# Quantizing the down-projection weights later in a cross-attention and FP4 feed-forward kernel

## The reference

```python
def fp4_quant_dequant(x):                     # blocks of 16 along the last axis
    scale = jnp.maximum(jnp.max(jnp.abs(xb), -1, keepdims=True) / 6.0, 1e-12)
    idx = jnp.searchsorted(_MID, jnp.abs(xb / scale))
    return (_GRID[idx] * jnp.sign(xb) * scale).reshape(shape)
def fp4_linear(x, w):
    return jnp.einsum('bsk,nk->bsn', fp4_quant_dequant(x), fp4_quant_dequant(w))
...
corr = jnp.real(jnp.fft.ifft(Qf * jnp.conj(Kf))).mean(axis=(0, 1))   # over all sequences
W_topk, I_topk = jax.lax.top_k(corr, 12); W_topk = softmax(W_topk)
R = sum(w * roll(v, -shift)); x = x + R @ Wout + bout
...
gate = fp4_linear(ln(x), w_gate); y = fp4_linear(ln(x), w_up)       # 256 -> 704
x = x + fp4_linear(silu(gate) * y, w_down)                           # 704 -> 256
```

## Time and profile before

| | us |
|---|---|
| median of 3 runs | 575.65 (574.96 to 576.95) |
| the profiled execution | 575.05 |
| its span, first to last instruction | 573.2 |
| busy: TensorE, VectorE, ScalarE, GpSimd | 466.7, 461.9, 393.3, 282.7 |

### The profile page before, as it was taken

The page is one execution under the profiler, slowest core; times in us unless marked ns, Lnnn a source line. Parts: engine busy times, 40 slices in busy tenths (PEclk is TensorE's granted clock), DMA queues, the critical chain, the costliest instruction groups (busy, mean ns, idle before and its releaser), DMA issues. The chain is left out here.

```text
span 573.2 us, 10039 instructions
## 1 busy us (share of the span) xinstructions
PE 466.7 (81%) x3454; PEld 306.1 (53%) x3454; DVE 461.9 (81%) x742; ACT 393.3 (69%) x666; POOL 282.7 (49%) x365
## 2 busy tenths in 40 slices
PE   5086798704789999999899999999899999999944
PEld 5075687501345565556555555556555565556633
DVE  2899864315799999999899999999899999998760
ACT  2177865535778777788888777788888778776530
POOL 3045351035356666656556666656556666632221
PEclk9689999775989999999999999999999999999987
DMA  9956550043145556555655557645655556544533
GB/s 283 344 170 202 176 186 14 25 102 75 37 97 122 110 122 127 120 106 111 128 118 119 110 123 126 121 107 110 130 116 119 112 115 110 108 88 98 88 78 78
DMA packets 165042, 69.19 MB, mean 121 GB/s; under 512 B 129152, under 2 KB 164736, under 8 KB 164992
## 3 DMA queue, kind: packets, MB, share of 16 engines
q1 hardware_dynamic: 164416, 68.03, 52.2%
q10 hardware_dynamic: 576, 0.53, 0.3%
HBM read 27.90 MB, written 9.18 MB: 65 GB/s over the span
## 5 line engine op out<-in xcount | busy, mean ns | idle before, releaser
L694 PE MATMUL ps<-guT_hi,a_xT 128*128 128x512 f16 (+1 forms) x384 | 140.7, 366 | 55.2 <-DMA a_xT<-ctx_sb 55.2
L405 POOL TENSOR_TENSOR ctx_sb<-h_c,sl 128x704 f16<-128x704 f16 x64 | 96.1, 1523 | 115.8 <-DVE ctx_sb L909 115.8
L704 PE MATMUL ps<-dT_hi,hqT 128*128 128x256 f16 x704 | 132.2, 276 | 12.3 <-DMA hqT<-ctx_sb 12.3
L696 PE MATMUL ps<-guT_hi,a_xT 128*128 128x512 f16 (+1 forms) x384 | 140.3, 365 | 0.0
L695 PE MATMUL ps<-guT_lo,a_xT 128*128 128x512 f16 (+1 forms) x384 | 140.1, 365 | 0.0
L694 PEld LDWEIGHTS ps<-guT_hi,a_xT 128*128 128x128 f16 x384 | 37.7, 98 | 103.7 <-DMA a_xT<-ctx_sb 46.0
L457 ACT ACTIVATE h_c<-y_h 128x1408 bf16<-128x1408 bf16 (+3 forms) x40 | 49.2, 1230 | 61.9 <-DVE y_h L939 36.5
L706 PE MATMUL ps<-dT_lo,hqT 128*128 128x256 f16 x384 | 89.6, 277 | 0.0
L704 PEld LDWEIGHTS ps<-dT_hi,hqT 128*128 128x128 f16 x704 | 69.7, 99 | 25.2 <-DMA hqT<-ctx_sb 13.1
L443 POOL TENSOR_TENSOR xs<-xs,w_raw 128x512 f32<-128x512 f32 x32 | 37.8, 1180 | 79.5 <-issue 49.6
L904 DVE SCALAR_TENSOR_TENSOR hb<-ps,h_in,w_raw 128x704 f32<-128x704 f32 x64 | 60.5, 945 | 4.7 <-PE ps L696 4.6
(11 more groups left out here) (139 smaller groups left out, 868.8 us busy)
## 6 DMA issues: line engine op xcount, KB each, us to landing
w_raw<-a_scratch SPq DMA_DIRECT2D x64, 128.5 KB, 2.6
xs<-in_x_dram SPq DMA_DIRECT2D x16, 512.0 KB, 5.3
ctx_sb<-in_ctx_dram SPq DMA_DIRECT2D x16, 512.0 KB, 4.4
out_dram<-a_xT SPq DMA_DIRECT2D x64, 128.0 KB, 2.0
hqT<-ctx_sb SPq DMA_TRANSPOSE x64, 3.7
w_raw<-in_L_ffn_w_down_dram SPq DMA_DIRECT2D x1, 704.0 KB, 8.1
w_raw<-in_L_ffn_w_gate_dram SPq DMA_DIRECT2D x1, 640.0 KB, 5.9
w_raw<-in_L_ffn_w_up_dram SPq DMA_DIRECT2D x1, 640.0 KB, 7.1
```

The source lines that it names most:

```text
L405: pool.tensor_tensor(hq[:, j % 2, t, FF:2 * FF].rearrange("p (ih r) -> p ih r", ih=IH), h_c[:, :].bitcast(F16).rearrange("p (ih t r) -> p ...
L694: pe.matmul(dst, xt[:, c, :], guT[0][:, c, n0:n1], start=(c == 0), stop=False)
L696: last = pe.matmul(dst, xt[:, KC + c, :], guT[0][:, c, n0:n1], start=False, stop=(c == KC - 1))
L704: pe.matmul(dst, hqT[:, j % 4, c, :], dT_hi[:, c, :], start=(c == 0), stop=False)
```

## The change

Gate and up, and down, are quantized as two parts, each with its own preparation (`w_prepare(part)`), its own largest value over the partitions (`largest(part)` on GpSimd) and its own factors (`w_scales(part)`).

- The load of the down weights is issued after the inputs of all steps, with a semaphore of its own, ahead of the late small loads.
- In the reading stage only the six pieces of gate and up are quantized (`N_GU` = 6).
- Down: `w_prepare(1)` stands on VectorE after the last `evac_qk` and ahead of the sums over Wout. The factors, both `w_segment` and the output factor with `ident_out` stand after the softmax's last operation; both `w_split` on ScalarE behind the eighth evacuation, ahead of the table load. `w_finish` of the two pieces stands at the end of VectorE's steps -2 and -1, `w_hi` on ScalarE in steps -1 and 0 ahead of the pair's normalization, `w_lo` at the end of GpSimd's steps -1 and 0. Their products lie in `d_prod`, a part of the buffer that held ctx.
- TensorE's five fills of down come in the tile loop: two after tile 2's gate and up, three after tile 3's, in turn through banks 6 and 7. ScalarE evacuates all five in step 1, after the SiLU of tile 3 and ahead of the rounding of x.
- The waits for all fills ahead of the products wait for eight; the first down product waits for 13. The small operations on the factors count on `c_steps` instead of `w_steps`.

```diff
-            down_v = w_raw[:, 256 * GU_CH:WCOLS].rearrange("p (c n) -> p c n", n=FF)
-            sp.dma_start(down_v, w_down.rearrange("(c p) n -> p c n", p=P)).then_inc(s["w_loaded"], 16)
             for i in range(2, NQ):
                 load_x(i)
                 load_c(i)
+            down_v = w_raw[:, 256 * GU_CH:WCOLS].rearrange("p (c n) -> p c n", n=FF)
+            sp.dma_start(down_v, w_down.rearrange("(c p) n -> p c n", p=P)).then_inc(s["d_loaded"], 16)
...
+            def largest(part):
+                pool.wait_ge(s["w_steps"], 2 + part * seg_at(N_GU - 1) + part * K_W)
+                pool.partition_all_reduce(w_pow[:, part:part + 1], w_max[:, part:part + 1], P, RMAX).then_inc(s["w_pool"], 1)
...
-            evacuate_weights(act, range(EARLY, len(FILLS)))
+            evacuate_weights(act, range(EARLY, GU_FILLS))
+            w_split(N_GU)
+            w_split(N_GU + 1)
             act.preload_act_table(ACT.Silu)
...
                 if tile_ok(2 * st - LAG - 1):
                     residual(2 * st - LAG - 1)
+                if st in (-1, 0):
+                    w_hi(N_GU + 1 + st)
...
                 if tile_ok(2 * st + 1):
                     silu(2 * st + 1)
+                if st == 1:
+                    evacuate_weights(act, range(GU_FILLS, len(FILLS)))
...
+                if i == 2:
+                    pe.wait_ge(s["w_lo"], len(SEGS))
+                for f in {2: range(GU_FILLS, GU_FILLS + 2), 3: range(GU_FILLS + 2, len(FILLS))}.get(i, ()):
+                    transpose_weights(f)
+                if i == LAG:
+                    pe.wait_ge(s["w_ev"], len(FILLS))
                 if tile_ok(i - LAG):
                     down(i - LAG)
...
+            def w_prepare(part):
+                cols = cols_of(part * N_GU)[0]
+                at = part * (seg_at(N_GU - 1) + K_W)
+                dve.wait_ge(s["d_loaded"] if part else s["w_loaded"], 16 if part else 16 * N_PIECES)
+                dve.tensor_reduce(w_bm[:, cols], w_raw[:, BLK * cols.start:BLK * cols.stop].rearrange("p (b i) -> p b i", i=BLK),
+                                  AX.X, ALU.max, apply_absolute_value=True).then_inc(ws, 1)
...
+            w_prepare(1)
             dve.wait_ge(s["late_loaded"], 32)
...
+            w_scales(1)
+            w_segment(N_GU)
+            w_segment(N_GU + 1)
+            dve.tensor_scalar(inv_out[:, :], w_inv[:, 1:2], h_tmp[:, 1:2], None, ALU.mult).then_inc(cs, 1)
...
+            dve.tensor_scalar(ident_out[:, :], ident[:, :], out_fac[:, 0:1], None, ALU.mult).then_inc(s["id_out"], 1)
...
+                if st in (-2, -1):
+                    w_finish(N_GU + 2 + st)
```

More of the change, by code:

```diff
@@ L50 @@
 AHEAD = 4
-W_FIRST = 0
 SLOT = P // QT
@@ L215, in chunks_of, with product, runs_of, scratch @@
             return w[:, o:o + n].rearrange("p (c ih r) -> p c ih r", ih=IH, r=r)
-        def runs_of(w, g):
+        def product(g):
+            o, n = SEGS[g]
+            return (hb if g < N_GU else d_prod)[:, FF * (g % 2):FF * (g % 2) + n]
+        def runs_of(g):
             o, n = SEGS[g]
             r = RUN_H if n == FF else RUN_X
-            return w[:, FF * (g % 2):FF * (g % 2) + n].rearrange("p (ih c r) -> p c ih r", ih=IH, r=r)
+            return product(g).rearrange("p (ih c r) -> p c ih r", ih=IH, r=r)
+        def scratch(w, g):
+            o, n = SEGS[g]
+            return w[:, FF * max(0, g - N_GU):FF * max(0, g - N_GU) + n]
+        def seg_at(g):
+            return 7 + K_W * g + (7 if g >= N_GU else 0)
+        def scaled_at(g):
+            return seg_at(g) + 1 if g <= N_GU else seg_at(g) - 2
+        def finish_at(g):
+            return seg_at(g) + (2 if g == N_GU else 1)
         def pair_ok(n):
@@ L249, in evacuate_weights @@
                 eng.wait_ge(s["w_tr"], f + 1)
-                src = bank16(f % 4)
+                src = bank16(f % 4 if f < GU_FILLS else 6 + f % 2)
                 if kind == "gu":
@@ L637, in transpose_weights @@
                 kind, part, a, b = FILLS[f]
-                need(pe, s["w_ev"], f - 3)
-                dst = bank16(f % 4)
+                need(pe, s["w_ev"], f - 3 if f < GU_FILLS else f - 1)
+                dst = bank16(f % 4 if f < GU_FILLS else 6 + f % 2)
                 if kind == "gu":
@@ L668, in _ @@
             pe.matmul(bank(4)[:, 0:P], ones[:, :], dg[:, :], start=True, stop=True).then_inc(s["t_pe"], 1)
-            for f in range(EARLY, len(FILLS)):
+            for f in range(EARLY, GU_FILLS):
                 transpose_weights(f)
@@ L734, in grid, with cols_of @@
                 return dve.tensor_tensor(c.bitcast(F16), c.bitcast(BF16), t.bitcast(F16), ALU.subtract)
+            def cols_of(g):
+                return (slice(0, n_gu), 0) if g < N_GU else (slice(n_gu, WCOLS // BLK), 1)
             def w_segment(g):
@@ L739, in w_segment @@
                 nb, b0 = n // BLK, o // BLK
-                at = 7 + K_W * g
+                at = seg_at(g)
                 shape = [P, IH, nb, 2]
                 runs = "p (ih b il) -> p ih b il"
-                y = y_h[:, 0:n]
-                need(dve, s["w_split"], 3 * g)
+                y = scratch(y_h, g)
+                need(dve, s["w_split"], 3 * min(g, N_GU))
                 dve.tensor_tensor(y.rearrange(runs, ih=IH, il=2),
@@ new lines, in w_scales @@
+            def w_scales(part):
+                one = slice(part, part + 1)
+                at = part * (seg_at(N_GU - 1) + K_W)
+                dve.wait_ge(s["w_pool"], part + 1)
+                dve.tensor_scalar(w_pow[:, one].bitcast(U32), w_pow[:, one].bitcast(U32), 0x7F800000, None, ALU.bitwise_and
+                                  ).then_inc(ws, 1)
+                dve.wait_ge(ws, at + 5)
+                dve.tensor_scalar(w_inv[:, one], w_pow[:, one], 2.0 ** -50, 2.0 ** -13, ALU.max, ALU.mult).then_inc(ws, 1)
+                dve.wait_ge(ws, at + 6)
+                dve.reciprocal(w_fac[:, one], w_inv[:, one]).then_inc(ws, 1)
@@ L826, in _ @@
                     evac_qk(i - 1)
[L827 to L832 removed]
+                if i == 0:
+                    w_scales(0)
+                if 0 <= i - 1 < N_GU:
+                    w_finish(i - 1)
+                if 0 <= i < N_GU:
+                    w_segment(i)
@@ L847, in _ @@
-            dve.wait_ge(ws, wend + 5)
-            dve.reciprocal(out_fac[:, :], inv_out[:, :]).then_inc(ws, 1)
-            dve.wait_ge(ws, wend + 6)
-            dve.wait_ge(s["trx"], 2 * NQ)
-            dve.tensor_scalar(ident_out[:, :], ident[:, :], out_fac[:, 0:1], None, ALU.mult).then_inc(s["id_out"], 1)
+            w_prepare(1)
             dve.wait_ge(s["late_loaded"], 32)
```

111 lines of the change are left out of this document (49 added, 62 removed).

## The result

The changed kernel takes 571.86 us (median of 7 runs, 570.98 to 573.28) against 576.95 (7 runs, 574.74 to 579.31) of the kernel before. The ratio is 0.991, with a 95% interval of 0.988 to 0.9939. The profiled span went from 573.2 to 569.2 us. The forecast was 572.1, faster. It was worked out from a median of 575.65 for the kernel before; beside these runs that kernel has 576.95.

A forecast was written before the change was run, and what follows sets the result against it. The prediction took the feed-forward, a closed loop of VectorE and ScalarE of 12.90 us, as the bound. Its terms, -3.3 - 3.75 + 0 + 1.3 + 2.2 = -3.55 us, took the median 575.65 to 572.1 us, range 570.3 to 574.9.

The forecast's parts named there:

- Start: Start of the reading stage: no wait for the down weights and a shorter preparation bring 3.3 us.
- 0.66 us pass: Start of the reading stage: time from the end of VectorE's reduction to GpSimd's maximum, putting that maximum at 18.1.
- rival (A): GpSimd also pays ahead of each maximum: the first 0.5 us later, 0.7 showing after the second; 573.3 us, chance 0.1.
- Rest of reading: Reading steps 7 to 9: without the two down pieces they need 11.19 us instead of 14.94, gain 3.75.
- Softmax: Softmax stage: the moved preparation, scalings and roundings fit into waits; 0, between -0.7 and +1.2 us.
- First finish: Start of the feed-forward: finishing the first down piece delays the next pair's normalization; cost 1.3 us, between 1.0 and 2.0.
- Evacuations: ScalarE, step 1: five evacuations of 4.07 us against 1.85 of cover cost 2.2 us, between 2.0 and 3.0.
- The loop: Feed-forward: the closed loop of VectorE and ScalarE keeps its cycle of 12.90 us.
- Rival (D): Feed-forward loop: shifted start brings a GpSimd collision in each cycle; 0.2 us a cycle gives 578.3 us, chance 0.07.
- (B): Prologue costs more: evacuations 3.0, first finish 2.0, softmax slip 0.5; 574.1 us, no measurable change, chance 0.15.
- (C): Evacuations find more cover or the first finish is free: half of 3.5 us of costs goes; 570.3 us, chance 0.1.
- (E): Start: another load, not the down weights, held it; only 1.5 of the 3.3 us come; 573.9 us, chance 0.03.

The follow-up runs named there:

- a: The changed kernel with the down weights' load issued ahead of the later inputs again, nothing waiting for it before the softmax stage; median 572.96 us, ratio 0.994.
- b: As a, and in addition the first preparation waits for the down weights; median 574.44 us, ratio 0.9957.
- d: The changed kernel with both down finishes moved behind the attention bias on VectorE and both high halves behind ScalarE's four attention DMAs; median 571.46 us.
- the doubled reduction: The changed kernel with the block maxima of the down weights taken twice on VectorE; median 572.9 us, ratio 0.9931.
- k_best: h without its wait ahead of VectorE's low halves, and with more unread TensorE products in the reading stage; median 567.38 us, ratio 0.9825.
- Experiment 3: The changed kernel with GpSimd's maximum over the partitions replaced by a copy of each partition's own value; median 572.69 us, ratio 0.9938.
- c: The kernel of Experiment 3: the changed kernel with a copy in place of GpSimd's maximum over the partitions; median 572.69 us, ratio 0.9938.
- g: The changed kernel plus unread TensorE transposes of the identity in the softmax stage and ahead of tile 0; median 568.72 us, ratio 0.9837.
- experiment 4: The changed kernel with the second reduction of 1408 columns (down weights' block maxima) done twice on VectorE; median 572.9 us, ratio 0.9931.
- Experiment 5: A repeat of the changed kernel, median 572.5 us, and d, with the down finishes and high halves moved earlier, median 571.46 us.
- h: e_all_early with VectorE's low halves held back until GpSimd's statistics of pair 0 are done, plus unread TensorE products in all stages; median 570.71 us, ratio 0.9875.
- j: As h, with the maximum spread by TensorE instead of GpSimd and step 1 evacuated ahead of the first rounding; median 570.07 us, ratio 0.9855.
- Experiment 6: As d, with low halves on VectorE, all down transposes ahead of tile 0, evacuations spread over ScalarE's waits; median 571.74 us, ratio 0.9909.
- experiment 2: As a, with the first preparation also waiting for the down weights; median 574.44 us, ratio 0.9957.
- e_all_early: The kernel of Experiment 6: as d, with all down weights transposed ahead of tile 0 and low halves on VectorE; median 571.74 us, ratio 0.9909.

## Why the prediction was right, step by step

**Start: forecast -3.3, measured -2.53.** The landing was right within 0.2 us (14.63 against 14.4) and the reduction within 0.1. What failed is "0.66 us pass" to the maximum: it came at 18.73, 0.64 us after VectorE's maximum had ended at 18.09, and 7.54 us after GpSimd's last work. In a, b, d and the doubled reduction, where VectorE is ready at 18.45 or later, the row is prompt (0.13 us); in k_best it comes 1.39 us after its data, 8.70 after GpSimd's earlier work. Nowhere does it start less than 7.03 us after that work. That is the first half of rival (A), with its 0.5 us. Behind it GpSimd took 8.32 us to its next operation, 0.8 more than the 7.53 of the earlier trace rows; over all runs with the maximum this time is 7.3 to 8.3. So VectorE waited 1.86 us for it. The second half of (A) didn't come: in the softmax stage the maximum starts 0.13 us after its data, [8.09 <-DVE w_s L839], since GpSimd had long been idle. Experiment 3 shows that the time behind belongs to this instruction: with a copy in its place it is gone. For the time ahead it can't tell, since there the data came only at 18.67. The Trainium skill (GPSIMD Engine Reference, "Instruction dispatch") gives about 6 us for the first call of a newly loaded routine, with no visible instruction. The traces agree in kind and show 7.0 to 8.7 us, in front of the maximum and behind it, and that the time in front runs while GpSimd waits. That it is such a load is the page's word; no trace names it.

**Rest of reading: forecast -3.75, measured -3.75.** Steps 7 to 9 took 53.88 to 65.07, 11.19 us, as worked out; the pace of 3.73 is there from step 7 on. After and its repeat have no fall of the clock in these steps. Four kernels do (a, b, c and g, of which g has the very same reading stage), and there it takes 1.6 us of the gain back (c). No forecast could count on either.

**Softmax: forecast 0, measured -0.41 to a_sb and -0.65 behind it.** All covers held. The second preparation fitted (experiment 4: 0.6 us to spare), and the scalings left 1.85 of the 4.91 us. Of the 0.41, 0.32 lie in TensorE's sixteen attention products, 5.11 us before and 4.79 after. (With the four over Wout in front they are twenty; the prediction speaks of eight.) Both sets start at half clock and end at full, and the clock is what makes the one shorter. Stretches of half clock in either, from the first of the sixteen on, before and then after:

```profile
110.77:113.65 2.88, 2.88 (x8) 2.22 (x8) 0.85 (x2) 0.39 (x1) 0.00 (x0) 0.50 0.00 0
```

```profile
104.41:106.60 2.19, 2.19 (x6) 1.67 (x6) 0.57 (x2) 1.48 (x2) 0.00 (x0) 0.50 0.00 0
```

That is 0.7 us less at half clock, and half of it is the 0.3. The forecast's bounds for this place, -0.7 to +0.7, held it. The 0.65 lies in the DMA round trip of the attention rows, which takes 3.9 to 5.0 us from the last a_sb to the first residual in the runs; I count it as no effect of the change; that is argued, not shown.

**First finish: forecast +1.3, measured +0.96,** just under the lower bound of 1.0. (The prediction's own terms give 130.2 + 0.79 - 129.56 = 1.4, not 1.3.) The mis-sized term is the finish of 2.35 us. The piece took 0.52 + 0.53 + 0.89, without the contention that is in the 2.35. Experiment 5 moved it away and got 0.94 back at the first gate product. The contention showed at the second piece: its last operation took 1.75 us, and that was absorbed, as predicted. It was even better than that by 0.33, and that is the clock again: tile 0 runs at half clock for its first 3.3 us in after, for its first 4.0 before. In the kernels without a stretch of half clock there (g, h, j, k) the first gate product and y_h(0) lie 11.96 to 11.98 us apart; in the others that figure is larger by half of the time at half clock, to 0.1 us (b 2.7 us and 13.27, after 3.3 and 13.56, before 4.0 and 13.89, the doubled reduction 5.9 and 14.87).

**Evacuations: forecast +2.2, measured +2.73.** The mis-sized term is their length, 4.07 us in the old place: in the new one they need 4.49 (150.56 to 155.05), as TensorE's transposes wait for free banks (3.82 us before the first row at 151.62) and go at the low clock, which is granted from 151.0 on (bounds 2.0 to 3.0, and this is why the upper one was there). Experiment 6 took them out of this place and the interval was 12.90 again.

**The loop: no change, right.** After's cycles are 12.90 us throughout. The kernel before has one of 13.26 (from 434.74), so the lead is 4.34 us at the last y_h; behind it, where the loop runs out, 0.34 are lost again. I count neither as an effect of the change. Rival (D) came true nowhere in after. Longer cycles do exist, in before and in five of the experiments' kernels; the one of 13.91 us that was looked into comes from TensorE's clock (experiment 6), not from the collision that (D) names.

**Sum: forecast -3.55, measured -4.0 by the spans.** The errors are +0.8, 0, -1.1, -0.3, -0.3 and +0.5; they cancel in part. The medians differ by 5.1 us, the ratio allows 3.5 to 6.9. That the time itself was met within 0.3 us is luck in part: the median of before lay 1.3 us higher beside these runs than in the forecast, and -3.55 from there would have given 573.4. Rivals (B), (C) and (E) are out: costs of 3.7 us together, not 5.5 or 1.8, and the wait for the down weights did set the start (experiment 2: about 1.8 us).

What no step of the forecast had is the role of TensorE's clock. It was counted at one place with 0 ("these products ran at the low level before too"), which was right for the difference to within 0.3 us at either place and missed that 3.1 us lay there for both kernels.

## What to carry over

Work moved into a wait costs nothing only if nothing that is waited for stands behind it in the order of its engine: name what each moved instruction stands in front of (the normalization behind an evacuation, here 2.7 us), not only how long the wait is. Before a difference of a microsecond between two traces is put down to an edit, look for the times at which the clock was low and at which a load was issued: they moved as much here with edits elsewhere. And when an engine's waits in a chain are long, look at the clock at which it works behind them: about a hundred unread transposes brought 3.1 us in the two intervals behind them, more than any other edit on top of the changed kernel.

## What the runs showed of the hardware

- The maximum over the partitions on GpSimd is 0.38 us of work, but where its data was there in time it started 7.0 to 8.7 us after GpSimd's earlier work, and it took 7.3 to 8.3 us to the next ordinary operation. With a copy in its place the second time is gone.
- The granted clock of TensorE is 0.50 or 1.00, and 0.50 was seen behind stretches in which TensorE had waited; with unread transposes in them it stayed at or went back to 1.00 earlier (99 to 107 us: 0.52 without, 1.00 with). Falls of 3.4 us in the reading stage cost 1 to 1.6 us each and come and go with edits elsewhere, so two kernels that differ by one edit can differ by that much for another reason. One in the loop cost 1.0 us of a cycle, though VectorE and ScalarE set the loop's pace.
- VectorE's low halves (two inputs, 704 columns) and GpSimd's addition of 512 columns stretch each other, as their rows in e_all_early overlap: GpSimd's 1.17 us became 1.62, and its addition of 2 columns, 0.20 us alone, became 0.84.
- A load of 64 KB from a scratch in memory (dg) took 1.7 to 1.9 us in twelve kernels, 2.5 in h_all_keep and 3.7 in j_all_keep; its cause is open.
